# Split products for a banded attention, the last rounding on GpSimd, and a new order at the end

## What is computed

```python
# banded attention: token t sees the 16 tokens before it, sigmoid instead of softmax
q = (x @ wq.T).reshape(B, T, H, HD)
kv = (x @ wkv.T).reshape(B, T, H, 2 * HD)
nb_k, nb_v = ...                       # keys and values of tokens t-1 .. t-16
tau = sigmoid(einsum('bthd,bthwd->bthw', q, nb_k) / SCALE)
y = x + einsum('bthw,bthwd->bthd', tau, nb_v).reshape(B, T, D) @ wo.T
out = layernorm(y) * gamma + beta

# feed-forward with ternary weights and tokens rounded to 8 bits
def act_quant(x):
    scale = 127.0 / clip(max(abs(x)), 1e-05)
    return clip(round(x * scale), -128.0, 127.0) / scale
h = silu(act_quant(x) @ ternary(w_gate).T) * (act_quant(x) @ ternary(w_up).T)
x + act_quant(h) @ ternary(w_down).T
```

## Time and profile before

| what | us |
|---|---|
| median of 3 runs (lowest, highest) | 641.39 (638.94, 642.73) |
| profiled execution, its own time | 644.46 |
| its span from first to last instruction | 641.6 |
| TensorE busy in the span | 575.8 (90%) |
| VectorE busy | 348.5 (54%) |
| ScalarE busy | 281.5 (44%) |
| GpSimd busy | 117.9 (18%) |
| mean granted TensorE clock | 0.971 of full speed |

### The profile page before, as it was taken

The page is one execution under the profiler, slowest core; times in us unless marked ns, Lnnn a source line. Parts: engine busy times, 40 slices in busy tenths (PEclk is TensorE's granted clock), DMA queues, the critical chain, the costliest instruction groups (busy, mean ns, idle before and its releaser), DMA issues.

```text
span 641.6 us, 13698 instructions
## 1 busy us (share of the span) xinstructions
PE 575.8 (90%) x5806; PEld 429.4 (67%) x5806; DVE 348.5 (54%) x672; ACT 281.5 (44%) x498; POOL 117.9 (18%) x124
## 2 busy tenths in 40 slices
PE   2899997999999889899998989999898969999856
PEld 1476654798776546888776657987666547997624
DVE  3876534457555443466544454675553343663687
ACT  2154443534245434533445436342554536445523
POOL 5331100012233100012423000122312000243010
PEclk9999997999999998999999999999999978999978
DMA  8710010010400200010501100104000100000000
GB/s 334 319 36 1 3 67 3 4 67 2 194 5 2 91 11 1 13 57 2 197 2 35 67 4 2 67 2 167 33 2 2 66 4 2 2 2 1 2 0 33
DMA packets 4547, 30.49 MB, mean 48 GB/s; under 512 B 1137, under 2 KB 1649, under 8 KB 2674
## 3 DMA queue, kind: packets, MB, share of 16 engines
q1 hardware_dynamic: 4466, 29.35, 12.0%
HBM read 28.82 MB, written 0.52 MB: 46 GB/s over the span
## 4 chain that ended last, share of the span: by engine, by line
PE 78%; DVE 9%; ACT 7%; issue 4%; POOL 1%; DMA 1%; POOLq 0%; DVEq 0%; ACTq 0%
PE psD L326 17%; PE QD L622 12%; PE psD L635 9%; PE QD L408 7%; PE QD L443 4%; PE psD L320 3%; ACT PTR L1239 3%; PE QD L436 3%; PE QD L394 3%; DVE AQ L1757 2%; PE QD L431 2%; PE psD L463 2%; PE psD L359 2%; PE psD L470 2%; PE psD L484 2%
## 5 line engine op out<-in xcount | busy, mean ns | idle before, releaser
L1239 ACT ACTIVATE PTR<-QD 128x2048 f32<-128x2048 f32 x40 | 75.1, 1878 | 44.9 <-PE QD L443 22.7
L2427 POOL TENSOR_TENSOR rstd<-ms,mhalf 128x2 f32<-128x2 f32 x26 | 19.6, 756 | 292.1 <-DVE ms L1696 291.7
L326 PE MATMUL psD<-WAB,hT 128*128 128x256 f32 (+1 forms) x216 | 69.4, 461 | 3.0 <-DVE hT L1711 3.0
L1757 DVE TENSOR_REDUCE AQ<-QD 128x8 f32<-128x2048 f32 (+1 forms) x24 | 55.0, 2291 | 30.4 <-PE QD L408 30.4
L622 PE MATMUL QD<-HH,WFH 128*128 128x256 f32 x224 | 67.4, 301 | 3.4 <-DVE HID L1874 1.7
L1858 DVE TENSOR_TENSOR WFL<-WC,WFH 128x512 fp32r<-128x512 f32 x64 | 48.0, 754 | 33.9 <-ACT WFH L1284 33.7
L1754 DVE TENSOR_REDUCE AQ<-QD 128x16 f32<-128x2048 f32 x16 | 36.7, 2293 | 53.2 <-PE QD L408 53.2
L622 PE MATMUL QD<-HL,WFH 128*128 128x256 f32 x224 | 63.3, 283 | 0.0
L622 PE MATMUL QD<-HH,WFL 128*128 128x256 f32 x224 | 63.3, 283 | 0.0
L635 PE MATMUL psD<-WC,HID 128*128 128x256 f32 x256 | 58.2, 380 | 0.0
L326 PEld LDWEIGHTS psD<-WAB,hT 128*128 128x128 f32 x216 | 39.3, 193 | 20.6 <-issue 12.8
(11 more groups left out here) (168 smaller groups left out, 1029.2 us busy)
## 6 DMA issues: line engine op xcount, KB each, us to landing
WC<-in_wc SPq DMA_DIRECT2D x4, 3072.0 KB, 11.2
WAB<-in_wa SPq DMA_DIRECT2D x4, 1024.0 KB, 5.0
WAB<-in_wb SPq DMA_DIRECT2D x4, 1024.0 KB, 4.8
WF<-in_wf SPq DMA_DIRECT2D x1, 3072.0 KB, 22.8
bias<-in_bias SPq DMA_DIRECT2D x4, 512.0 KB, 3.9
WAB<-in_wt SPq DMA_DIRECT2D x1, 1024.0 KB, 4.8
X<-in_x SPq DMA_DIRECT2D x1, 512.0 KB, 3.6
out_x<-X SPq DMA_DIRECT2D x4, 128.0 KB, 1.7
```

Source lines behind the costliest of these rows:

```text
L326: mm = pe.matmul(bank(l, use)[:, col:col + n], lhs(k), rhs(k), start=(k == 0), stop=(k == KT - 1))
L1239: nc.scalar.activation(PTR[:, r % 2, :], QD[:, :], ACT.Exp, scale=SCALE).then_inc(t_exp, 1)
L1757: v = dve.tensor_reduce(QKR[b][:, t, 0, h, MAXROW].rearrange("p (s r) -> p r s", r=SG_H), QD[:, :].rearrange("p (r s n) -> p r s n", r=4, ...
```

## The change

- The banded attention's queries, keys and values are made from split weights and split tokens, in the buffers of the hidden units. ScalarE's `window_high(w)` makes the three weights' high parts, GpSimd's `window_low(w)` their low parts, VectorE's `window_T` the tokens' high part and the new `window_T_low` the low part. The queries of sequence 0 are now made before its keys.
- `round_hidden(t)` moves from VectorE to GpSimd and no longer clamps at 127; VectorE's `hidden_T` clamps at both ends.
- The scale that the rounding needs is announced before the scale of the output is computed (`out_scale_set`).
- The calls of all engines from the last layer's feed-forward on stand in a new order, the largest move being that sequence 1's messages and output projection (`window_pv(1, 1)`, `out_proj` with "mwo1") go ahead of the quantised products.

```diff
             ("ln_var", "ln_rstd", "an_set", "xn_set", "beta_set", "xq_set"))
+        wt_high, wt_low, an_high = sem("wt_high"), sem("wt_low"), sem("an_high")
         v_step = sem("v_step")
...
         qg_full, qg_free, qu_full, qu_free = sem("qg_full"), sem("qg_free"), sem("qu_full"), sem("qu_free")
+        out_scale_set = sem("out_scale_set")
         gq_scale_set, gq_scaled = sem("gq_scale_set"), sem("gq_scaled")
...
                 use = ("wq", "wk")[w] + str(b)
-                pe.wait_ge(wt_ld, 16)
-                pe.wait_ge(*emptied(NL, f"an{b}"))
                 next_bank(NL, use)
                 pe.wait_ge(*free_for(NL, use))
-                for m in range(KT):
-                    mm = project(NL, use, m * L, lambda k: Wt[:, w, k, m * P:(m + 1) * P], lambda k: hT[b][:, k, :])
+                pe.wait_ge(an_high, b + 1)
+                pe.wait_ge(wt_high, w + 1)
+                for part in range(3):
+                    if part == 1:
+                        pe.wait_ge(wt_low, w + 1)
+                    elif part == 2:
+                        pe.wait_ge(*emptied(NL, f"an{b}"))
+                    wp, hp = ((w_high(w), HH), (w_low(w), HH), (w_high(w), HL))[part]
+                    for m in range(KT):
+                        for k in range(KT):
+                            mm = pe.matmul(bank(NL, use)[:, m * L:(m + 1) * L], wp[:, 2 * k + m, :], hp[:, k, :],
+                                           start=(part == m == k == 0), stop=(part == 2 and k == KT - 1), skip_group_check=True)
                 mm.then_inc(full(NL, use), 1)
+            def window_values(use, b, tiles):
+                next_bank(NL, use)
+                pe.wait_ge(*free_for(NL, use))
+                pe.wait_ge(wt_low, 3)
+                pe.wait_ge(*emptied(NL, f"an{b}"))
+                for n, at in enumerate(tiles):
+                    for k in range(KT):
+                        for part, (wp, hp) in enumerate(((WFH, HH), (WFL, HH), (WFH, HL))):
+                            mm = pe.matmul(bank(NL, use)[:, n * D:(n + 1) * D], hp[:, k, at:at + P], wp[:, 2, k * D:(k + 1) * D],
+                                           start=(n == k == part == 0), stop=(k == KT - 1 and part == 2), skip_group_check=True)
+                mm.then_inc(full(NL, use), 1)
             def window_v(b):
-                pe.wait_ge(*emptied(NL, f"an{b}"))
-                next_bank(NL, f"wv{b}")
-                pe.wait_ge(*free_for(NL, f"wv{b}"))
-                for t in range(QT):
-                    mm = project(NL, f"wv{b}", t * D, lambda k: hT[b][:, k, t * P:(t + 1) * P], lambda k: Wt[:, 2, k, :])
-                mm.then_inc(full(NL, f"wv{b}"), 1)
+                window_values(f"wv{b}", b, (0, P))
...
-                next_bank(NL, f"wm{b}")
-                pe.wait_ge(*free_for(NL, f"wm{b}"))
-                project(NL, f"wm{b}", 0, lambda k: hT[b][:, k, P // 2:P // 2 + P], lambda k: Wt[:, 2, k, :])\
-                    .then_inc(full(NL, f"wm{b}"), 1)
+                window_values(f"wm{b}", b, (P // 2,))
...
             down(NL - 1, 1, range(4, FT))
+            window_qk(0, 0)
             window_qk(0, 1)
-            window_qk(0, 0)
             window_v(0)
...
             window_pv(1, 0)
+            window_pv(1, 1)
             rounded_T(0)
+            out_proj(NL, 1, "mwo1", Wt[:, 3, :, :], "pw1")
             quantised_gate_up(0, 0)
             quantised_gate_up(0, 1)
-            window_pv(1, 1)
             quantised_gate_up(1, 0)
-            out_proj(NL, 1, "mwo1", Wt[:, 3, :, :], "pw1")
-            hidden_T(0)
             quantised_gate_up(1, 1)
...
             quantised_gate_up(3, 0)
+            hidden_T(0)
             quantised_gate_up(3, 1)
             hidden_T(1)
+            hidden_T(2)
             quantised_down(0)
-            hidden_T(2)
             quantised_down(1)
...
                                      ACT.Abs, accum_out=asum[:, n:n + 1]).then_inc(asum_set, 1)
+            def window_high(w):
+                if w == 0:
+                    act.wait_ge(wt_ld, 16)
+                    act.wait_ge(*hidden_full(NL - 1, 1, FT - 1))
+                nc.scalar.activation(WFH[:, w, :], WT[:, w * KT * D:(w + 1) * KT * D], ACT.Copy).then_inc(wt_high, 1)
...
             gate(NL - 1, 0, 5)
+            gate(NL - 1, 0, 6)
             squares(NL - 1, 2, 1)
-            gate(NL - 1, 0, 6)
             split_high(NL - 1, 10)
             gate(NL - 1, 0, 7)
-            ternary(0)
             squares(NL, 0, 0)
+            gate(NL - 1, 1, 0)
             split_high(NL - 1, 11)
-            gate(NL - 1, 1, 0)
+            gate(NL - 1, 1, 1)
             split_high(NL - 1, 12)
-            gate(NL - 1, 1, 1)
             split_high(NL - 1, 13)
             gate(NL - 1, 1, 2)
+            gate(NL - 1, 1, 3)
             split_high(NL - 1, 14)
-            gate(NL - 1, 1, 3)
+            gate(NL - 1, 1, 4)
             split_high(NL - 1, 15)
-            gate(NL - 1, 1, 4)
+            ternary(0)
             gate(NL - 1, 1, 5)
...
             gate(NL - 1, 1, 7)
-            ternary(1)
+            window_high(0)
+            window_high(1)
+            sigmoid_table()
+            window_high(2)
             squares(NL, 0, 1)
-            sigmoid_table()
             window_q(0)
-            ternary(2)
             window_v(0)
...
             window_v(1)
+            ternary(1)
             sigmoids(3)
+            copy_oT(NL, 1, "pw1")
+            ternary(2)
             silu_table()
...
             quantised_gates(0, 1)
-            copy_oT(NL, 1, "pw1")
             quantised_gates(1, 0)
-            ternary(3)
-            scale_hidden(0)
             quantised_gates(1, 1)
             quantised_gates(2, 0)
+            scale_hidden(0)
             quantised_gates(2, 1)
+            quantised_gates(3, 0)
+            ternary(3)
             scale_hidden(1)
-            quantised_gates(3, 0)
             quantised_gates(3, 1)
...
                 done(dve.tensor_scalar(a[:, t:t + n, 3], a[:, t:t + n, 0], 1e-5, 1.0 / 127.0, ALU.max, ALU.mult))
-                done(dve.reciprocal(a[:, t:t + n, 2], a[:, t:t + n, 3]))
+                return dve.reciprocal(a[:, t:t + n, 2], a[:, t:t + n, 3])
...
                 dve.wait_ge(*filled(NL, f"an{b}"))
-                dve.tensor_copy(hT[b][:, :, :].rearrange("p k n -> p (k n)"), bank(NL, f"an{b}")[:, :])\
-                   .then_inc(free(NL, f"an{b}"), 1)
+                if b == 0:
+                    dve.wait_ge(*hidden_full(NL - 1, 1, FT - 1))
+                else:
+                    for use in ("wq0", "wk0", "wv0", "wm0"):
+                        dve.wait_ge(*filled(NL, use))
+                dve.tensor_copy(HH[:, :, :].rearrange("p k n -> p (k n)"), bank(NL, f"an{b}")[:, :]).then_inc(an_high, 1)
+            def window_T_low(b):
+                dve.wait_ge(an_high, b + 1)
+                dve.tensor_tensor(HL[:, :, :].rearrange("p k n -> p (k n)"), bank(NL, f"an{b}")[:, :],
+                                  HH[:, :, :].rearrange("p k n -> p (k n)"), ALU.subtract).then_inc(free(NL, f"an{b}"), 1)
...
                 ts = (2 * b, 2 * b + 1)
-                quantise_scales(b * 2, 2, hs[:, 2 * b:2 * b + 2, :], 0)
+                done(quantise_scales(b * 2, 2, hs[:, 2 * b:2 * b + 2, :], 0))
                 for t in ts:
...
                 dve.wait_ge(qu_free, 2 * t + 2)
-                quantise_scales(t, 1, GU(t).unsqueeze(1), 1)
-                dve.tensor_scalar(sgu[:, t, 2:3], am2[:, t, 3:4], mw[:, 2:3], None, ALU.mult).then_inc(gq_scale_set, 1)
-            def round_hidden(t):
-                dve.wait_ge(gq_scaled, t + 1)
-                dve.tensor_scalar(GQ(t), GU(t), MAGIC, 127.0, ALU.subtract, ALU.min).then_inc(gq_set, 1)
+                quantise_scales(t, 1, GU(t).unsqueeze(1), 1).then_inc(gq_scale_set, 1)
+                dve.tensor_scalar(sgu[:, t, 2:3], am2[:, t, 3:4], mw[:, 2:3], None, ALU.mult).then_inc(out_scale_set, 1)
...
                 dve.wait_ge(*filled(NL, f"gT{t}"))
-                dve.tensor_scalar(GQT(t), bank(NL, f"gT{t}")[:, :].bitcast(BF16), -128.0, None, ALU.max)\
+                dve.tensor_scalar(GQT(t), bank(NL, f"gT{t}")[:, :].bitcast(BF16), -128.0, 127.0, ALU.max, ALU.min)\
                    .then_inc(free(NL, f"gT{t}"), 1)
...
             def output(t):
-                dve.wait_ge(gq_scale_set, t + 1)
+                dve.wait_ge(out_scale_set, t + 1)
                 dve.wait_ge(*filled(NL, f"d{t}"))
...
             residual(NL - 1, 1, "cwo1")
+            split_low(NL - 1, 8)
+            mean_square(NL - 1, 2, 1)
             hidden(NL - 1, 0, 5)
-            mean_square(NL - 1, 2, 1)
             hidden(NL - 1, 0, 6)
...
             hidden(NL - 1, 0, 7)
-            split_low(NL - 1, 8)
+            split_low(NL - 1, 9)
             weigh_T(NL - 1, 2, 1)
...
             tokens_low(NL - 1, 1)
-            split_low(NL - 1, 9)
+            residual(NL - 1, 0, "y0")
             split_low(NL - 1, 10)
```

(76 more changed lines are left out.)

## The result

The changed kernel takes 645.06 us (median of 9 runs, 641.85 to 649.06) where the kernel before takes 641.76 beside it (9 runs); the ratio is 1.0061, interval 1.0041 to 1.0082. The forecast was 638.4. Run again later, the change gave 644.81 against 641.65, ratio 1.0042 (1.0017 to 1.0068). So it costs 3.2 to 3.3 us; the forecast had it gaining 2.95. (The ratios and intervals are those on record; they needn't be the quotient of the two medians.)

A forecast was written before the change was run, and what follows sets the result against it. TensorE's work bounds up to 597 us, then VectorE's order and what waits for it; -1.6 products, -3.7 earlier sequence 1, +0.7 VectorE, -0.1 tail, +1.7 clock give -2.95 unrounded: 638.4, range 635.6 to 641.9.

The forecast's parts named there:

- the price of a rounding on GpSimd: Roundings of the gated columns, 128x1024: 1.07 us each on GpSimd, half the scaling's 1.99 plus 0.07, against 0.69 on VectorE.
- tail at full clock: Work after the last scale, from scaling to output: -0.1 us in the sum, from rounding +0.4 and faster products.
- only the last rounding is on the path: Of the four GpSimd roundings only the last lengthens the path, +0.4 us; the other three can hold VectorE.
- the slower rival: GpSimd's rounded-output weight subtractions, between 572 and 578, exceed 1.3 us; beyond 1.9, 3 us delay per us; up to 646.9; chance 0.09.
- TensorE never waits for them: GpSimd's weight subtractions, 1.3 us each, end at 573.3, 577.2 and 578.4, before products ask at 578.0, 579.5 and 580.4.
- Split products: Queries, keys and values: 0.36 us instead of 0.432 a product, 1.6 us gained ahead of sequence 0's output projection, preparation mostly hidden.
- The order: Sequence 1's projection goes before the feed-forward: its sum at 607.25 instead of 613.20, rounded tokens 5.3 us earlier.
- The hidden units' +0.2: GpSimd's scaling moved behind the power frees unit 11 and can hold 12 or 13: 0.18 lost instead of 0.36.
- VectorE gives back 0.7: After sequence 1's rounded tokens: VectorE's backlog and one hold cost +0.7 us, leaving 4.6 of 5.3 at the last scale.
- Holds of reductions: VectorE's reductions beside GpSimd roundings: taken as not held; rival, held, 1.8 us later at half clock, 639.6, chance 0.10.
- Clock: Half clock from about 612 to 632 after a 4.5 us idle stretch and gaps: +1.7 us in the tail.
- the full-clock rival: TensorE's bursts from 590 to 607 suffice to keep the clock full: gain 4.7 us, 636.7; chance 0.24.

The follow-up runs named there:

- m1: Whole computation left out: single GpSimd operations timed alone, then VectorE steps started just behind one; subtracting one constant from 128x1024 took 2769 ns with float32 output.
- m2: Whole computation left out: nine forms of GpSimd operations timed alone; multiply by a column and add took 1.12 us, multiply by a column and subtract 3.71.
- e7: e2 with GpSimd's rounding written as multiply by a column of ones, add the negative constant: 635.59 us against 641.18 for the kernel before, ratio 0.9910.
- e2: Changed kernel with GpSimd's zeroing of the value pads moved ahead of the power of layer norm 2: 640.74 us, ratio 0.9980 to the kernel before.
- e4: e2 with GpSimd's rounding written as multiply by a column of ones, subtract the constant: 642.01 us against 641.65 for the kernel before, ratio 1.0021.
- e5: e3 with queries, keys and values in float32 products, so without the split: 639.36 us, ratio 0.9966 to the kernel before; again 640.24, 0.9965.
- e3: Changed kernel with the zeroing earlier and the four roundings back on VectorE: 639.37 us, ratio 0.9985 to the kernel before; again 639.06, 0.9951.

## Why the prediction was wrong

**The step that failed: the price of a rounding on GpSimd.** It was put at 1.07 us, from the scaling's 1.99; it took 2.75 to 2.78. The scaling multiplies by a column and adds a constant, the rounding subtracts a constant, and these are not of one price (1.12 and 2.77 in m1 and m2). The sum had "tail at full clock" at -0.1 and +1.7 for half clock in it, so +1.6; measured from last maximum to end it was +4.4, 2.8 too much. Its parts show beside e7, whose tail of 6.01 is about that of before: in the changed kernel block 2's scaled values are ready at 625.96 (ScalarE's row at 624.82 + 1.14) and its transposes start at 629.99, 4.0 later, since its rounding stands in GpSimd's queue until 627.2 and then takes 2.75; in e7 the same distance is 1.3. That is 2.7. The other 1.7 is clock: from the start of these transposes to the start of the last ones' products it takes 5.13 us at mostly half clock, and 3.39 in e7. Together 4.5, which rounded is the difference of the two tails (10.51 and 6.01). The dose bears it out: roundings of 1.12, 2.77 and 3.70 us give tails of 6.0, 10.3 and 12.2 us (e7, e2, e4), and nothing else in these kernels differs, though the granted clock of the tail differs with it.

The prediction also thought that only the last rounding is on the path. That holds while one is shorter than the distance of two scale searches on VectorE, 2.77 us (reductions at 623.07 and 625.84 in the changed kernel). At 2.75 GpSimd has no slack: a rounding that starts late hands it to the next.

I had asked of the other new operation, the two-tile subtraction, what it costs if its form has no row, and made it the slower rival. It takes 1.26, as priced. The same question was due for the rounding, whose form had no row either; the only upper bound I gave it was 0.5 to 0.9 us by the Trainium skill's page GPSIMD Engine Reference, section Elementwise — side-by-side cycle accounting. The sign of the result came by a mechanism that no rival held.

**The second step that failed: a term put at nothing, GpSimd's hold on the norming.** "TensorE never waits for them" was true of the subtractions' results and false of their side effect. The subtraction came when it was laid: 1.3 ahead of 573.3 in before's times is 25.0 from the mark, and it began at 25.0 (567.23). VectorE's norming pair stood there already in before (572.10, 25.1 from the mark) and began at 24.65 in the changed kernel. So the sum had both at one place and no term for their meeting. Cost: 3.6 us on VectorE, 2.28 of TensorE idle, +2.1 at T0 in the table, and in two of three traces 1.7 more by the clock. The prediction knew that such a step is held for a whole instruction (2.48 in the earlier trace rows) and looked for holds among the hidden units' low parts and the scale steps alone.

**How much each was.** From the mark the forecast's end is at 89.5 (636.55) and its last maximum at 81.7 (before's 86.29 less 4.6). The changed kernel has 95.3 and 84.79: of the 5.8 us too much, 3.1 stand ahead of the tail, where e2, in which the hold is short, has 81.81, and 2.7 in the tail. So the two steps weigh about the same. A third term was off the other way: the time around the span was kept as in before (2.4 to 2.9 at the median), and the changed kernel has 1.8.

**Split products: right.** 1.4 us from T0 to sum 0 in the first trace, and 1.5 between e5 and e3, against 1.6; and 0.12 for a product. The preparation stayed hidden but for the hold.

**The order: right up to the last scale.** Its sum of sequence 0 was laid at 595.6, which is 48.6 from the mark, and tokens 1 at 70.0; e2 has 48.50 and 70.50. Sequence 1's sum was laid at 60.2 and came at 61.0. The hidden units' +0.2 came as 0.4 at T0 in e2 (26.62 against 26.99). That VectorE gives back 0.7 of this before the last scale came out as 1.1 in the changed kernel (tokens 2.56 ahead of before's, last maximum 1.50), 0.6 in e2 and 1.3 in e7. At the end, with the roundings on VectorE and no split, the order alone had little left in the traces (92.00 and 92.66 against 92.42).

**Holds of reductions: right.** Reductions and 128x1 steps ran unheld beside roundings; the one hold of 0.36 that I allowed didn't appear.

**Clock: half right.** The forecast had half clock from 612 to 632, which is 65 to 85 from the mark. In the changed kernel it stood at 0.50 from 611 to 621, 69 to 79 from the mark, came back to 0.98, and was at 0.50 again from 629 to 633, behind the idle stretch that the roundings made; in e7 it stayed at 1.00 from 623 on. So the +1.7 in the tail was there in the changed kernel, but not by the forecast's reason, the gaps before dense work, and it is absent in e7.

What the change would take with the fast form alone wasn't run. An estimate is e7's 635.59 plus what the earlier zeroing is worth: 2.45 at T0, 4.3 between the medians of the changed kernel and e2, so 638.0 to 639.9. The lower end is near the forecast's 638.4, and that would be luck: the hold was missing from the sum, and e7's full clock (its end at 88.49 from the mark, where the full-clock rival had 87.8) gives back the 1.7 that the forecast had taken.
